# Low-rank second products from gathered adapter rows: one matmul per block instead of two

## The chip, the cores and the metric

The kernel runs on one core of a Trainium2 chip. Its metric is the device time of one execution in microseconds (us). Before the change the median of 3 runs is 657.62 us (656.94 to 659.66); the execution that was profiled took 656.7 us.

The engines are TensorE (PE, with its weight loads as PEld), VectorE (DVE), ScalarE (ACT), GpSimd (POOL) and SyncE (SP, which here only issues DMAs).

## The reference

Two layers, each a convolution or mixing followed by a residual feed-forward with low-rank parts, on x of 32 batches x 64 rows x 1024 columns, all in float32. Cut to what matters:

```
y   = einsum('bsd,od->bso', c0, weight) + bias        # c0: grouped convolution of x, plus a context term
seg = searchsorted(lora_start_indices, arange(B), side='right') - 1
a   = clip(seg - 1, 0, 2)                             # adapter of a batch, 3 adapters of rank 16
lo  = einsum('bsr,bor->bso', einsum('bsd,brd->bsr', c0, lora_A[a]), lora_B[a])
x   = x + y + where(seg > 0, lo, 0)                   # first layer
x   = x + second_layer(x)                             # 1x1 mixing by a softmax, scores, top 16 of 64 experts, A, gates, B
```

The change is in the product with `lora_B` and in the bias. Each batch has at most one of the three adapters.

## The kernel before

The 32 batches go in 4 groups of 8: 8 batches x 64 rows are 512 tokens, held as 4 blocks t of 128. Group 0 has its own code (`first_group`), groups 1 to 3 run `group`. A group's stages on PE are: the convolution; the first feed-forward product with weights of 128 x 1024 (pieces); the mixing and the scores; the experts' A product; the experts' B product. In groups 1 to 3 the feed-forward products go in seven block products (`winograd`, 24 matmuls each, numbered by their first step). To get float32 accuracy a product has three matmuls, high x high, high x low and low x high; ACT makes the high part of an operand (a copy into fp32r) and DVE the low part (a subtraction), so each piece passes SP (DMA), ACT, DVE and PE.

Every engine works its instructions off in the order in which its block of the source gives them, and waits on semaphores (`s_...`) written out by hand. The order is fixed; nothing is planned at run time.

The adapter part of a group:

- `lora_first` (L1392): 16 matmuls give the products with all three adapters, 48 rows twice (rows 0 to 47 with the high part of A, 64 to 111 with its low part), for 512 tokens in one bank.
- `masked` on DVE (L910) multiplies with `lora_mask`, which POOL computed in `adapters` (L573, 14 small operations): a row is kept where the batch has that adapter.
- `lora_parts` on ACT (L674) writes the high part to `lora_s1` (112 rows; row 48 is 1 for the bias) and a copy to the upper rows of `lora_s2`; `lora_rest` on DVE (L917) writes the low part to the lower rows of `lora_s2`.
- `lora_second` (L1399) adds the adapter part and the bias to a bank of the feed-forward product: two matmuls for a block t and a half h of the 1024 output columns, with `lora_m1` (high part of B over all 48 adapter rows, and the bias) and `lora_m2` (high and low parts). There are 8 blocks and halves in a group. In group 0 the 4 of h = 0 come after piece 3 of `ffn_piece` (L1484), those of h = 1 within piece 7, one after each t. In groups 1 to 3 two stand after winograd 8, two and two after winograd 10, two after winograd 12.

`const_hi` (ACT, L740) and `const_lo` (DVE, L1054) make `lora_m1` and `lora_m2` once, in group 0, out of the loaded `lora_b`.

POOL does little: memsets, `adapters()` (L621), then `mix_weights(0)` (L601, 15 operations over 128 x 256), and a loop over groups with `onto_diagonal` (L616), which sets the left side for the mixing stage, and `mix_weights(g + 1)`, which starts with the first second product of the group. In DVE's order the batch items of the convolution (`conv_item`, `conv_lo`) come first in a group; in group 1 DVE also has a combination of weights (`combine(3)`, `combined_lo(3, .)`) beside its usual work. `choose` is the selection of the top 16 experts.

Of the kernel before, what the change touches and what calls it, by code (L numbers as in the profile page):

```python
# [24 lines left out]
F32 = mybir.dt.float32  # L25
F32R = mybir.dt.float32r
I32 = mybir.dt.int32
ALU = mybir.AluOpType
# [3 lines left out]
P = 128  # L32
# [37 lines left out]
def adaln_ffn_kernel(nc, conv_x, x, taps, pieces, first_consts, hidden_w, later_consts, lora_a, lora_b,  # L70
                     starts, wr, expand, spread, out):
    with ExitStack() as ctx:
# [28 lines left out]
        lora_m1 = sb("lora_m1", [P, L], F32R)  # L101
        lora_m2 = sb("lora_m2", [P, L], F32R)
# [36 lines left out]
        lora_h, score_t, gate_t = small, small, small[0:KR_E, :]  # L139
        lora_a_raw = small[:, 0:PH * LORA].rearrange("p (k m) -> p k m", m=LORA)  # L140
# [67 lines left out]
        s_lora_lo = sem("s_lora_lo")  # L208
        s_ffn = sem("s_ffn")
# [21 lines left out]

        kept = nc.dram_tensor("kept", (16, 2, P, L), F32, kind="Internal").ap()
# [81 lines left out]
        def _(sp):  # L314
# [88 lines left out]
            def first_group():  # L403
# [14 lines left out]
                sp.wait_ge(s_const_hi, 4)  # L418
# [146 lines left out]
        def _(pool):  # L565
            pool.memset(ones[:, :], 1.0).then_inc(s_ones, 1)
            pool.memset(lora_a_r[:, :, :].bitcast(F32), 0.0).then_inc(s_ones, 1)
            pool.memset(lora_s2[:, :].bitcast(F32), 0.0).then_inc(s_ones, 1)
            pool.wait_ge(s_ones, 3)
            pool.memset(lora_s2[96:P, :].bitcast(F32), 1.0).then_inc(s_ones, 1)  # L570
            pool.wait_ge(s_ones, 4)

            def adapters():  # L573
# [25 lines left out]
                then(pool.tensor_scalar(lora_mask[:, :], high, 2.0, acol, ALU.subtract, ALU.is_equal))  # L599
# [21 lines left out]
            adapters()  # L621
            pool.wait_ge(s_att, 4)
# [3 lines left out]
            pool.wait_ge(s_ones, 5)  # L626
            for g in range(GROUPS):

                pool.wait_ge(s_conv, g * GB + 1)
                onto_diagonal()  # L630
                if g < GROUPS - 1:

                    pool.wait_ge(s_ffn, g * 8 + 1)
                    pool.wait_ge(s_bd, 2 * g + 2)
                    mix_weights(g + 1)

        @block.scalar
        def _(act):
# [74 lines left out]
            def first_group():  # L713
# [26 lines left out]
                def const_hi(n):  # L740
                    if n != 2:
                        act.wait_ge((s_lora_a, s_lora_b, None, s_wr)[n], 16)
                    if n == 0:
                        act.wait_ge(s_ones, 4)
                    to, of = ((lora_a_r[:, :, 0:LORA], lora_a_raw), (lora_m1[:, :], lora_b_stage),
                              (lora_m2[0:LORA_LO, :], x1[0:LORA_LO, 1, :]), (wr_r[:, :, 0:KR_E], wr_raw))[n]
# [24 lines left out]
                for n in range(1, 4):  # L771
                    const_hi(n)
# [5 lines left out]
                lora_parts(0)  # L778
                split_first(5)
# [47 lines left out]
            def group(g, last):  # L827
# [13 lines left out]
                lora_parts(g)  # L841
                next_split(8)
# [43 lines left out]
        def _(dve):  # L886
            dve.wait_ge(s_ones, 4)
# [29 lines left out]
            def lora_rest(g):  # L917
                dve.wait_ge(s_lora_s, 2 * g + 1)
                dve.wait_ge(s_lora_masked, g + 1)
                dve.tensor_tensor(lora_s2[0:LORA, :], lora_h[0:LORA, :], lora_s1[0:LORA, :].bitcast(F32),  # L920
                                  ALU.subtract).then_inc(s_lora_lo, 1)
# [93 lines left out]
            def first_group():  # L1015
# [12 lines left out]

                def softmax_max():
# [24 lines left out]
                def const_lo(n):  # L1054

                    dve.wait_ge(s_const_hi, (1, 2, 4)[n])
# [11 lines left out]
                for b in range(GB):  # L1068
# [9 lines left out]
                    if b == 1:  # L1078
                        rest_of_context()
                    if b == 4:  # L1080
# [15 lines left out]
                dve.wait_ge(s_adapter, 14)  # L1096
# [268 lines left out]
        def _(pe):  # L1365
# [33 lines left out]
            def lora_second(h, t, bank, start):  # L1399
                pe.matmul(banks[bank][:, :], lora_s1[0:LORA_M, t * P:(t + 1) * P],  # L1400
# [398 lines left out]
```

## Time and profile before

| what | value |
|---|---|
| median of 3 runs | 657.62 us (656.94 to 659.66) |
| profiled execution | 656.7 us, of which the span is 654.9 us |
| PE busy | 648.1 us (99%), 3197 matmul records |
| PEld busy | 537.7 us (82%) |
| DVE busy | 451.4 us (69%) |
| ACT busy | 214.0 us (33%) |
| POOL busy | 73.8 us (11%) |
| DMA | 157.98 MB, mean 241 GB/s |

Busy time is the time in which an engine has an instruction under way; the span is from the first to the last instruction. Matmuls overlap each other, so the mean duration of one (395 ns) is longer than the interval between two starts. The profile's clock row gives the TensorE clock that was granted, as a share of the full 2.4 GHz.

### The profile page before, as it was taken

What the parts mean: (1) busy time and instruction counts of PE and PEld (TensorE: products, weight loads), DVE (VectorE), ACT (ScalarE), POOL (GpSimd) and SP (SyncE); (2) the same over time, 40 slices, a digit from 0 to 9 for tenths busy, and PEclk for the clock granted to TensorE, in tenths of its full rate; (3) what the DMA queues carried; (4) which work ended last, traced back from release to release, by engine and by line L of the source; (5) the groups of instructions that cost most, each with busy time, mean ns of one, the idle gap of its engine ahead of it and who ended that gap; (6) DMA issues with size and microseconds to landing.
All of it is one profiled execution on the core that took longest, in us unless ns stands there. A gap on an engine that the chain in (4) does not pass through costs nothing.

```text
span 654.9 us, 8354 instructions
## 1 busy us (share of the span) xinstructions
PE 648.1 (99%) x3197; PEld 537.7 (82%) x3197; DVE 451.4 (69%) x690; ACT 214.0 (33%) x275; POOL 73.8 (11%) x91
## 2 busy tenths in 40 slices
PE   9999999999999999999999999999999999999997
PEld 8878888888897788888889788888879888888885
DVE  2859469549377788558769758636967856665785
ACT  2714135233144024335115312333423421433420
POOL 1598200000000160000000042000000000000000
PEclk9999999999999999999999999999999999999999
DMA  8587714986969926776976682287797664037795
GB/s 303 210 293 279 299 50 144 356 246 218 392 228 379 356 100 260 280 223 245 366 275 220 261 318 97 102 225 245 290 325 264 273 248 184 0 118 203 211 345 221
DMA packets 51594, 157.98 MB, mean 241 GB/s; under 512 B 5488, under 2 KB 6384, under 8 KB 51568
## 3 DMA queue, kind: packets, MB, share of 16 engines
q1 hardware_dynamic: 46240, 148.05, 62.7%
q10 hardware_dynamic: 5328, 9.61, 4.8%
q8 instruction: 13, 0.21, 0.1%
q14 instruction: 13, 0.11, 0.1%
HBM read 131.94 MB, written 25.71 MB: 241 GB/s over the span
## 4 chain that ended last, share of the span: by engine, by line
PE 91%; DVE 3%; DMA 3%; issue 1%; SPq 1%; ACT 0%; DVEq 0%
PE bank L1374 25%; PE bank L1376 24%; PE bank L1375 24%; PE bank L1388 9%; PE bank L1408 3%; DMA piece_lo<-kept 2%; PE bank L1395 2%; PE bank L1414 1%; PE bank L1402 1%; PE bank L1400 1%; PE bank L1415 1%; DVE x L925 1%; DMA gate<-hidden_w 1%; DVE u_lo L1012 1%; DVE work L932 1%
## 5 line engine op out<-in xcount | busy, mean ns | idle before, releaser
L893 DVE TENSOR_TENSOR piece_lo<-raw,piece_hi 128x1024 fp32r<-128x1024 f32 x60 | 74.1, 1239 | 90.0 <-ACT piece_hi L647 89.8
L647 ACT ACTIVATE piece_hi<-raw 128x1024 fp32r<-128x1024 f32 x60 | 63.4, 1058 | 147.1 <-PE bank L1376 103.2
L1374 PE MATMUL bank<-piece_hi,u_hi 128*128 128x512 f32 x272 | 107.9, 397 | 0.0
L1376 PE MATMUL bank<-piece_hi,u_lo 128*128 128x512 f32 x272 | 107.3, 395 | 0.0
L1375 PE MATMUL bank<-piece_lo,u_hi 128*128 128x512 f32 x272 | 107.3, 394 | 0.0
L1374 PE MATMUL bank<-v_hi,piece_hi 128*128 128x512 f32 x256 | 101.8, 398 | 0.0
L1376 PE MATMUL bank<-v_hi,piece_lo 128*128 128x512 f32 x256 | 101.1, 395 | 0.0
L1375 PE MATMUL bank<-v_lo,piece_hi 128*128 128x512 f32 x256 | 101.0, 394 | 0.0
L1374 PE MATMUL bank<-piece_hi,v_hi 128*128 128x512 f32 x192 | 76.0, 396 | 0.8 <-DMA piece_lo<-kept 0.8
L1376 PE MATMUL bank<-piece_hi,v_lo 128*128 128x512 f32 x192 | 75.8, 395 | 0.0
L1375 PE MATMUL bank<-piece_lo,v_hi 128*128 128x512 f32 x192 | 75.8, 395 | 0.0
L652 ACT ACTIVATE u_hi<-work 128x512 fp32r<-128x512 f32 x64 | 40.1, 631 | 87.6 <-DVE work L988 50.8
L925 DVE TENSOR_TENSOR x<-x,bank 128x512 f32<-128x512 f32 x86 | 54.3, 679 | 17.0 <-PE bank L1402 12.7
L1374 PEld LDWEIGHTS bank<-piece_hi,u_hi 128*128 128x128 f32 x272 | 51.2, 188 | 12.4 <-issue 0.5
L1376 PEld LDWEIGHTS bank<-piece_hi,u_lo 128*128 128x128 f32 x272 | 51.2, 188 | 12.0
L1375 PEld LDWEIGHTS bank<-piece_lo,u_hi 128*128 128x128 f32 x272 | 51.2, 188 | 11.8
L1388 PE MATMUL bank<-toep,conv_in 128*128 128x128 f32 x512 | 59.2, 276 | 0.2 <-DMA toep<-taps 0.2
L1388 PEld LDWEIGHTS bank<-toep,conv_in 128*128 128x128 f32 x512 | 58.2, 192 | 0.8 <-DMA toep<-taps 0.4
L1376 PEld LDWEIGHTS bank<-v_hi,piece_lo 128*128 128x128 f32 x256 | 48.2, 188 | 11.5
L1375 PEld LDWEIGHTS bank<-v_lo,piece_hi 128*128 128x128 f32 x256 | 48.2, 188 | 11.0
L1374 PEld LDWEIGHTS bank<-v_hi,piece_hi 128*128 128x128 f32 x256 | 48.2, 188 | 10.9
L899 DVE TENSOR_TENSOR u_lo<-work,u_hi 128x512 fp32r<-128x512 f32 x64 | 43.7, 686 | 15.1 <-ACT u_hi L652 13.8
(143 smaller groups left out, 800.7 us busy)
## 6 DMA issues: line engine op xcount, KB each, us to landing
raw<-pieces SPq DMA_DIRECT2D x76, 512.0 KB, 5.5
piece_hi<-kept SPq DMA_DIRECT2D x48, 512.0 KB, 4.7
piece_lo<-kept SPq DMA_DIRECT2D x48, 512.0 KB, 5.8
x<-x SPq DMA_DIRECT2D x16, 512.0 KB, 5.3
gate_x<-gates ACTq DMA_DIRECT2D x32, 256.0 KB
out<-x SPq DMA_DIRECT2D x32, 256.0 KB, 4.8
conv_in<-conv_x SPq DMA_DIRECT2D x15, 516.0 KB, 7.1
conv_in<-pieces SPq DMA_DIRECT2D x12, 512.0 KB, 8.8
```

The lines of the kernel that those rows point to most:

```text
L647: act.activation(piece_hi[:, n % SLOTS, :], raw[:, r % RAWS, :], ACT.Copy).then_inc(s_piece_hi, 1)
L652: act.activation(to, of, ACT.Copy).then_inc(s_hi, 1)
L893: dve.tensor_tensor(piece_lo[:, n % SLOTS, :], raw[:, r % RAWS, :], piece_hi[:, n % SLOTS, :].bitcast(F32), ALU.subtract).then_inc(s_piece ...
L899: dve.tensor_tensor(to, of, hi, ALU.subtract).then_inc(s_lo, 1)
L925: dve.tensor_tensor(half, half, of, ALU.add).then_inc(done, 1)
L932: dve.tensor_tensor(work[:, c, :], banks[bank][:, :], mixb_bc[:, :, :].rearrange("p b c -> p (b c)"), ALU.add).then_inc(s_item, 1)
L1374: pe.matmul(to, left_hi, right_hi, start=first, stop=False)
L1375: pe.matmul(to, left_hi, right_lo, start=False, stop=False)
L1376: return pe.matmul(to, left_lo, right_hi, start=False, stop=last)
L1388: mm = pe.matmul(banks[bank][:, cg * P:(cg + 1) * P], conv_in[:, b, cg, h:h + Q], toep[:, cg, 1 - h, :], start=(h == 0), stop=(h == 1))
L1395: mm = pe.matmul(banks[bank][0:LORA_M, :], lora_a_r[:, k, :], part[:, k, :], start=(k == 0 and part is u_hi), stop=(k == NCH - 1 and part ...
L1408: mm = pe.matmul(banks[bank][:, t * P:(t + 1) * P], x1[:, t, c * P:(c + 1) * P], blockdiag[:, t, :], start=True, stop=True)
```

## The change

The products with `lora_B` take one matmul instead of two. Its left side, `lora_s1`, has 128 rows, 64 for the even and 64 for the odd batches of each block, of which a batch fills its own 64 and leaves the others zero. The 64 rows of a batch are: 16 x 3 for its one adapter (the parts that meet the high, the low and the high part of B), and two for the bias. A matmul with a matrix of zeros and ones (`place`, 128 x 112, built by POOL in the tile of `ones`) puts the rows of `lora_s2` there, and two ACT copies bring them from the bank to `lora_s1`. The right side is `lora_m`, four slots of 128 x 512, each filled by an indirect DMA from a table in DRAM (`lora_rows`, 2 halves x 160 rows x 512) by row numbers that POOL computes from the batches' adapters. POOL writes the table by 12 DMAs. A slot is filled for one block t and one half h, and filled again when the matmul that reads it is done: 8 gathers of 256 KB a group, 32 in all. DVE computes a row number's base (`row_numbers`) after its second convolution item.

```diff
+            def placement():
+                first, second = agg_part[:, 0, 0:RANK], agg_part[:, 0, RANK:2 * RANK]
+                halves = place_r[:, :].rearrange("p (b j) -> p b j", b=2)
+                pool.wait_ge(s_p_att, 2)
+                pool.memset(place[:, :], 0.0).then_inc(s_place, 1)
...
+                pool.wait_ge(s_place, 7)
+            def store_rows():
+                pool.wait_ge(s_const_hi, 2)
+                pool.wait_ge(s_const_lo, 2)
+                for h in range(2):
...
+                    for part, rows in ((0, lora_m1[0:LORA, cols]), (1, lora_m2[LORA_LO:LORA_M, cols]),
+                                       (2, lora_m1[0:LORA, cols])):
+                        pool.dma_start(by_adapter[:, part * RANK:(part + 1) * RANK, :],
+                                       rows.bitcast(F32)).then_inc(s_rows, 16)
...
+                pool.wait_ge(s_rows, 16 * 12)
+            def gather(g, h, t, slot):
+                at = g * NT + t
+                pool.indirect_dma_start(lora_m[:, slot, :].bitcast(F32), None,
+                                        lora_rows.rearrange("h r n -> (h r) n"),
+                                        bass.IndirectOffsetOnAxis(ap=lora_row[:, at:at + 1], axis=0),
+                                        element_offset=h * 160 * HALF).then_inc(s_gather[slot], 16)
...
             adapters()
+            store_rows()
+            for t in range(NT):
+                gather(0, 0, t, (t + 2) % 4)
+            gathered(1)
+            placement()
             pool.wait_ge(s_att, 4)
             mix_weights(0)
...
                 onto_diagonal()
+                pool.wait_ge(s_bd, 2 * g + 2)
+                if g == 0:
+                    pool.wait_ge(s_ffn, 4)
+                    for t in range(NT):
+                        gather(0, 1, t, t)
+                    pool.wait_ge(s_ffn, 8)
+                else:
+                    for pair in range(2):
+                        pool.wait_ge(s_ffn, g * 8 + 2 * pair + 2)
+                        for s in range(2):
+                            gather(g, 1 - pair, 2 + s, 2 * pair + s)
                 if g < GROUPS - 1:
-                    pool.wait_ge(s_ffn, g * 8 + 1)
-                    pool.wait_ge(s_bd, 2 * g + 2)
+                    for pair in range(2):
+                        pool.wait_ge(s_ffn, g * 8 + 2 * pair + 6)
+                        for s in range(2):
+                            gather(g + 1, 1 - pair, s, 2 * pair + s)
+                    gathered(2 * g + 3)
                     mix_weights(g + 1)
...
             def lora_parts(g):
                 act.wait_ge(s_lora_masked, g + 1)
-                act.activation(lora_s1[0:LORA_M, :], lora_h[0:LORA_M, :], ACT.Identity,
-                               bias=ecol[0:LORA_M, 0:1]).then_inc(s_lora_s, 1)
-                act.activation(lora_s2[LORA_LO:LORA_M, :], lora_h[0:LORA, :], ACT.Copy).then_inc(s_lora_s, 1)
+                act.activation(lora_s2[0:LORA_LO, :], lora_h[0:LORA_LO, :], ACT.Identity,
+                               bias=ecol[0:LORA_LO, 0:1]).then_inc(s_lora_s, 1)
+            def lora_placed(g, bank):
+                act.wait_ge(s_lora_placed, g + 1)
+                for b in range(2):
...
+                    act.activation(lora_s1[rows, :].rearrange("p (t b c) -> p t b c", b=2, c=C)[:, :, b, :], of,
+                                   ACT.Copy).then_inc(s_lora_rows, 1)
...
+                def row_numbers():
+                    dve.wait_ge(s_later, 16)
...
-            def lora_second(h, t, bank, start):
...
+            def lora_place(g, bank):
+                pe.wait_ge(s_lora_lo, g + 1)
+                pe.matmul(banks[bank][:, :], place_r[0:LORA_M, :], lora_s2[0:LORA_M, :], start=True,
+                          stop=True).then_inc(s_lora_placed, 1)
+            def lora_second(gathered, t, slot, bank, start):
+                pe.wait_ge(s_gather[slot], gathered)
+                pe.matmul(banks[bank][:, :], lora_s1[:, t * P:(t + 1) * P], lora_m[:, slot, :], start=start,
                           stop=True).then_inc(s_ffn, 1)
...
+                        if n == 3 and t == NT - 1:
+                            pe.wait_ge(s_place, 7)
+                            lora_place(0, 5)
...
                     if n == 3:
-                        pe.wait_ge(s_lora_s, 2)
...
+                        pe.wait_ge(s_lora_rows, 2)
                         for t in range(NT):
-                            lora_second(0, t, t, False)
+                            lora_second(16, t, (t + 2) % 4, t, False)
```

Further edits: `adapters` gets 9 more operations on POOL, the row numbers (DVE waits for 22 counts of `s_adapter` instead of 14); `const_hi` loses one of its four ACT copies; `lora_rest` is two DVE operations instead of one; `lora_placed` stands behind `lora_parts` on ACT, in group 0 before `split_first(5)`, later before `next_split(8)`. In groups 1 to 3 the placement matmul stands between winograd 4 and winograd 6 and waits for `s_lora_lo`; PE waits for `s_lora_rows` before winograd 8. One of POOL's opening memsets goes.

## Rows read from the trace of the kernel before

**Rows 1.** Page, parts 1 and 2: PE's busy time, its granted clock.
```profile
PE 648.1 (99%) x3197; PEld 537.7 (82%) x3197; DVE 451.4 (69%) x690; ACT 214.0 (33%) x275; POOL 73.8 (11%) x91
PEclk9999999999999999999999999999999999999999
```

**Rows 2.** Page, part 4: the chain that ended last, by engine.
```profile
PE 91%; DVE 3%; DMA 3%; issue 1%; SPq 1%; ACT 0%; DVEq 0%
```

**Rows 3.** PE's waits: who waited, for whom, total us, times, longest.
```profile
PE bank L1374 <- DMA piece_lo<-kept: 0.8, 1, 0.8
```

**Rows 4.** Timeline of PE (start, duration in us): first and 25th matmul.
```profile
53.43 0.40 PE L1374 MATMUL bank<-piece_hi,u_hi 128*128 128x512 f32 x1
...
59.00 0.39 PE L1374 MATMUL bank<-piece_hi,u_hi 128*128 128x512 f32 x1
```

**Rows 5.** Stretches: PE, PEld, DVE, ACT, POOL busy, PE clock, DMA share.
```profile
226.00:232.00 6.00, 6.00 (x27) 4.86 (x27) 3.48 (x5) 1.06 (x1) 5.31 (x7) 1.00 0.79 317
240.00:258.00 18.00, 17.39 (x106) 14.89 (x105) 16.64 (x23) 8.59 (x13) 0.04 (x1) 1.00 0.57 223
```

**Rows 6.** Tile lora_s: duration ns min/median/max, first and last start us.
```profile
L1400 PE MATMUL bank<-lora_m,lora_s x32: 391/398/402, 51.6 to 554.6; 112*128 112x512 f32 x32
L676 ACT ACTIVATE lora_s<-small,consts x4: 723/724/726, 46.9 to 524.4; 112x512 fp32r<-112x512 f32 x4
```

**Rows 7.** Timeline of POOL in group 0.
```profile
17.46 0.42 POOL L586 CAST starts_f<-starts_i 128x4 f32<-128x4 int32 x1 [14.70 <-DMA consts<-later_consts]
...
25.45 0.93 POOL L599 TENSOR_SCALAR lora_mask<-left,consts 128x32 f32<-128x32 f32 x1
32.00 1.59 POOL L609 TENSOR_TENSOR agg<-att_pair,consts 128x256 f32<-128x256 f32 x1 [5.62 <-DVE att_pair L1048]
...
34.69 1.60 POOL L613 TENSOR_TENSOR agg<-agg,agg_part 128x256 f32<-128x256 f32 x1
...
47.23 0.74 POOL L613 TENSOR_TENSOR agg<-agg,agg_part 128x256 f32<-128x256 f32 x1
...
48.62 2.64 POOL L619 COPY blockdiag<-agg 64x256 f32<-64x256 f32 x2
```

**Rows 8.** Timeline of PE, and chain of waits: piece 3, mixing stage.
```profile
50.15 0.40 PE L1374 MATMUL bank<-piece_hi,u_hi 128*128 128x512 f32 x1
77.77 3.57 PE bank L1408 x32
```

**Rows 9.** Timelines of DVE and ACT in group 0.
```profile
14.93 0.67 DVE L903 TENSOR_TENSOR work<-bank,cond_bc 128x512 f32<-128x512 f32 x1
...
31.88 1.22 DVE L1060 TENSOR_TENSOR lora_m<-x,lora_m 64x1024 fp32r<-64x1024 f32 x1
26.07 1.99 ACT L747 ACTIVATE lora_m<-x 128x1024 fp32r<-128x1024 f32 x2
```

**Rows 10.** Timeline of SP's queue, and DMA issues (KB, us to landing).
```profile
3.42 0.43 SPq L390 DMA_DIRECT2D gate<-hidden_w  x1
gates<-small ACTq DMA_DIRECT2D x4, 128.0 KB, 2.6
out<-x SPq DMA_DIRECT2D x32, 256.0 KB, 4.8
```

**Rows 11.** Timeline of PE's weight loads at the start.
```profile
0.99 4.90 PEld L1370 LDWEIGHTS bank<-ones 128*128 128x128 f32 x24 [0.99 <-POOL ones L566]
5.81 0.97 PEld L1388 LDWEIGHTS bank<-toep,conv_in 128*128 128x128 f32 x8
```

**Rows 12.** The chain of waits, and the timeline of ACT, in group 2.
```profile
363.18 3.73 PE bank L1395 x16
369.72 1.06 ACT L647 ACTIVATE piece_hi<-raw 128x1024 fp32r<-128x1024 f32 x1 [0.68 <-PE bank L1376]
```

**Rows 13.** Timeline of DVE in groups 1 and 3, four x adds.
```profile
233.17 4.05 DVE L925 TENSOR_TENSOR x<-x,partial 128x512 f32<-128x512 f32 x4
547.53 2.49 DVE L925 TENSOR_TENSOR x<-x,partial 128x512 f32<-128x512 f32 x4
```

More of the change, by code:

```diff
@@ L27 @@
 I32 = mybir.dt.int32
+U32 = mybir.dt.uint32
 ALU = mybir.AluOpType
@@ L139, in adaln_ffn_kernel @@
         lora_h, score_t, gate_t = small, small, small[0:KR_E, :]
+        place = ones[:, :]
+        place_r = place.bitcast(F32R)
+        lora_m1, lora_m2 = (lora_m[:, 2 * n:2 * n + 2, :].rearrange("p s n -> p (s n)") for n in range(2))
         lora_a_raw = small[:, 0:PH * LORA].rearrange("p (k m) -> p k m", m=LORA)
@@ L208, in adaln_ffn_kernel @@
         s_lora_lo = sem("s_lora_lo")
+        s_lora_rest = sem("s_lora_rest")
+        s_lora_placed = sem("s_lora_placed")
+        s_lora_rows = sem("s_lora_rows")
+        s_gather = [sem(f"s_gather{slot}") for slot in range(4)]
+        s_row = sem("s_row")
+        s_rows = sem("s_rows")
+        s_place = sem("s_place")
         s_ffn = sem("s_ffn")
@@ L567, in _ @@
             pool.memset(lora_a_r[:, :, :].bitcast(F32), 0.0).then_inc(s_ones, 1)
[L568 to L571, printed above, removed]
+            pool.memset(lora_s1[:, :].bitcast(F32), 0.0).then_inc(s_ones, 1)
             def adapters():
@@ L598, in adapters @@
                 then(pool.tensor_tensor(high, high, low, ALU.add))
-                then(pool.tensor_scalar(lora_mask[:, :], high, 2.0, acol, ALU.subtract, ALU.is_equal))
+                then(pool.tensor_scalar(lora_mask[:, :], high, 2.0, acol, ALU.subtract, ALU.is_equal), False)
+                least_row, quarter_row, row = (stat[:, 1, n:n + 1] for n in range(3))
+                then(pool.tensor_scalar(low, high, 2.0, 0.0, ALU.subtract, ALU.max), False)
+                then(pool.tensor_scalar(least_row, acol, 3.0, 2.0, ALU.is_ge, ALU.mult), False)
@@ new lines, in adapters @@
+                then(pool.tensor_scalar(quarter_row, acol, 2.0, 32.0, ALU.is_ge, ALU.mult))
+                pool.wait_ge(s_row, 1)
+                then(pool.tensor_tensor(row, quarter_row, stat[:, 0, 0:1], ALU.add), False)
+                then(pool.tensor_scalar(low, low, least_row, 48.0, ALU.max, ALU.mult))
+                then(pool.tensor_scalar(low, low, row, None, ALU.add))
+                for b in range(2):
+                    rows = slice(b * C, (b + 1) * C)
+                    then(pool.tensor_copy(lora_row[rows, :], low[rows, :].rearrange("p (t b) -> p t b", b=2)[:, :, b]))
@@ new lines, in gather, with gathered @@
+            def gather(g, h, t, slot):
[4 more added lines that the diff above has]
+                                        element_offset=h * 160 * HALF).then_inc(s_gather[slot], 16)
+            def gathered(count):
+                for slot in range(4):
+                    pool.wait_ge(s_gather[slot], 16 * count)
@@ L770, in first_group @@
                         logits_exp()
-                for n in range(1, 4):
+                for n in range(1, 3):
                     const_hi(n)
@@ L778, in first_group @@
                 lora_parts(0)
+                lora_placed(0, 5)
                 split_first(5)
@@ L841, in group @@
                 lora_parts(g)
+                lora_placed(g, 0)
                 next_split(8)
@@ L1079, in first_group @@
                         rest_of_context()
+                        row_numbers()
                     if b == 4:
@@ L1674, in group @@
                 for s in range(2):
-                    lora_second(0, 2 + s, 1 - s, False)
+                    lora_second(g * 32 + 32, 2 + s, 2 + s, 1 - s, False)
                 def h_of(c, ks):
```

83 lines of the change are left out of this document (54 added, 29 removed).

## The prediction

> **What bounds the kernel now.** I read the page's first two parts, then the chain of waits, the waits of TensorE (PE), and the timelines of the places that the diff touches. PE is busy 99% of 654.9 us at a granted clock of 1.00 [rows 1]; the chain is PE's for 91% [rows 2]; PE's longest wait in the steady groups is 0.8 us [rows 3]. So a matmul that disappears is worth its issue interval, not its 395 ns (these overlap): 24 matmuls from 53.43 to 59.00 us [rows 4] make 5.57 / 24 = 0.232 us. For the same reason each wait that is new on PE counts in full; there is no slack for it to fall into. The one stretch that another engine sets is the mixing stage of group 1: in 240 to 258 us PE has 17.39 of 18.00 us and DVE 16.64 [rows 5].
>
> **What the change removes.** 64 second-product matmuls (two lines of 32, the first in [rows 6]) become 32, and one placement matmul comes with each of 4 groups: 28 fewer, 28 x 0.232 = 6.5 us, 1.6 us a group. On ACT two operations of which the longer has 0.72 us [rows 6] become one of that kind and two half-size copies; on DVE one operation becomes two. Weight and moving shapes stay near 128 x 512, so I keep the interval.
>
> **What it adds in group 0: a chain on POOL that PE waits for.** Now POOL ends the adapter masks at 25.45 + 0.93 = 26.4 us, mixes weights from 32.00 to 47.97, and PE wants nothing of it until the mixing stage at 77.77 [rows 7, 8]. After, the placement matmul (before the last quarter of piece 3) waits for s_place 7, and ahead of that on POOL stand, in order:
> - 9 more mask operations. 14 took 17.46 to 26.4, 0.64 each, so they end near 32.1. Hidden: the store waits longer.
> - The store waits for const_lo 1, on DVE at 31.88 + 1.22 = 33.1 [rows 9]. DVE itself is late: row_numbers waits after the second convolution item (14.93) for later_consts, which POOL sees at 17.46 [rows 7, 9]. DVE stops 2.5 us and its later gaps (it still waits three times for PE in this stage) win back half; one ACT copy less (half of 1.99 us for two, [rows 9]) wins back more. I take +0.8: the store starts at 33.9. On PE this costs up to 0.7 us at the last quarter of piece 0, but the stall below swallows it.
> - 12 DMA issues on POOL. No row shows one. Bounds: the 0.43 us of an SP issue, and the 1.60 us of a POOL add [rows 7, 10]. I take 1.0, the middle, since neither is nearer: 12.0 us, to 45.9. Then the last must land: 2.6 us is the fastest of the DMAs by kind [rows 10]; I take 3.0, near it, since these are small: 48.9.
> - 4 gathers (256 KB each) at 1.0, and landing. Bounds of landing: 2.6 and, for 256 KB, 4.8 us [rows 10]; since SP, whose loads wait for DVE, has little left to issue while PE stands, 3.0: 55.9.
> - 7 small operations at 0.3, half the 0.64 above since they are at most half as wide (the memset aside): 2.1 us. The placement is ready at T = 58.0.
> PE arrives at 50.15 [rows 8] and stalls 58.0 - 50.2 = 7.8 us. With both low ends T = 33.9 + 5.2 + 2.6 + 1.7 + 2.6 + 2.1 = 48.1: no stall. With the high ones T = 33.9 + 19.2 + 4.8 + 6.4 + 4.8 + 2.1 = 71.2: a stall of 21 us. Behind the waiting matmul PE has everything; ACT too waits in its order (lora_placed stands before split_first 5), and so does DVE.
>
> **A second stall of the same chain.** From T, PE has 1 + 6 + 4 + 3 x 24 + 6 = 89 matmuls, 20.6 us, to the first product of the second half, which needs slot 0 of the second gathers (the two ACT copies, about 0.45 each, are ready before the 6 matmuls are through). POOL has from T: mixing weights 16.0 (as now), memset and diagonal copies 3.3 [rows 7], one issue 1.0, landing 3.4: T + 23.7. PE stalls another 3.1, and ends the piece 22 matmuls later at T + 28.8 = 86.8, against 77.77 now: **+9.0 us in group 0**, the removed matmuls included.
> The granted clock is 1.00 in every row, but PE never stood for more than a microsecond, so no row shows a restart after 7.8 us of idleness. Nearest: the first 24 weight loads took 4.90 us, 0.204 each, the next 8 took 0.97, 0.121 each [rows 11]: a slow restart would lose at most 24 x 0.083 = 2.0 us, and here it would eat into the second stall. So 0 in the sum, 2.0 in the range.
>
> **Groups 1 to 3: the gathers.** A slot is free when the product that used it ends (R); the same slot is wanted 26 matmuls after the release, R + 5.9 us (slot 0 or 2) and R + 6.1 (slot 1 or 3). Issue 1.0, landing 4.0 (between 2.6 and 4.8; the DMA share is 0.79 at 226 to 232 us, [rows 5]): R + 5.1 and R + 6.1. So 0, just. With 1.6 and 4.8 the second comes at R + 8.1: 2.0 us a pair, two pairs a group, 12 us in all at the high end. The Trainium skill (DMA: Bandwidth & Descriptors, "Anatomy of one DMA") gives about 2.0 us plus the bytes at 436 GB/s for a DMA from GpSimd, an estimate of 2.6 us for 256 KB where the rows of this trace have 4.8; with 2.6 for every landing the sum would be 1.6 us lower.
> The gathered rows add 32 x 256 KB = 8.4 MB to 158 MB; PE's only DMA wait (0.8 us) may grow. I cost it 0.
>
> **ACT's order.** In group 2 ACT splits piece 8 at 369.72, while PE's first adapter product ends at 363.18 + 3.73 = 366.9 [rows 12] and winograd 4 24 matmuls later, at 372.5. After, lora_placed stands before both splits (pieces 8 and 9) and waits for PE at 372.5. Piece 8 is then split at 373.8 to 374.9, its rest on DVE at 376.1; PE wants it after 24 more matmuls, at 378.1. Piece 9: DVE's four adds between (2.5) put it at 379.8, wanted 12 matmuls on at 380.9. Hidden with 2.0 and 1.1 us to spare; cost 0, up to 1 a group if copies are slower.
>
> **POOL's mixing moved.** mix_weights(g+1) now runs beside the last second products, and it slows DVE: four x adds take 4.05 us beside it in group 1, 2.49 without it in group 3 [rows 13]: 0.4 each. After, it starts when the gathers have landed, some 8 us later, so beside the mixing stage. In groups 0 and 2 DVE has room: a chunk costs PE 8 short matmul records (32 are 3.57 us, [rows 8]) and 5 long ones, 0.89 + 1.16 = 2.05 us, and DVE two operations of 0.67 [rows 9], 1.7 with one of them slowed. In group 1, where DVE also has a weight combination, it gives back about what is won earlier: 6 + 3 operations, 0.4 us each, 3.6 us at most, against 2.2 us gained before and 1.6 of matmuls: I take 0 for this group, between -1.6 and +3. Groups 2 and 3 keep their 1.6: -3.2.
>
> **Sum.** +9.0 + 0 - 3.2 = +5.8 us. The profiled execution took 656.7 (its span 654.9 and 1.8 around it): 662.5. It lay 0.9 under the median of the runs, 657.6, so on the median's scale 663.4.
>
> **Rivals.**
> - Cheap issues on POOL: near 0.43 us each. For it: no POOL row has to do with a DMA, so nothing shows 1.0. Against it: 12 issues and two landings in a row must fit in 16 us. No stall: group 0 gives its 1.6 too, less 0.7 for DVE's wait: 657.6 - 0.9 - 3.2 = 653.5. Chance 0.13. This is the other side; it decides below (50.2 - 33.9 - 2.6 - 2.6 - 2.1) / 16 = 0.56 us an issue.
> - Issues about 0.65, and group 1 losing 2 to 3 us on DVE: T = 52.4, group 0 +3.4, the sum +2.2 to +3.2, 660 to 661. It needs two middling costs. Chance 0.13.
> - The gathers late in every group: issue 1.3 or more, T = 62.8 (group 0 +14) and 1 us at each of 6 pairs. For it: the margin above is zero. 657.6 + 14 - 3.2 + 6 = 674. Against: the gathers have 5.9 us where the DMA rows of that size have 4.8. Chance 0.17.
> - The forecast, 659 to 669: 0.57.
>
> **Numbers.** I can tell 0.5% (3.3 us) from nothing. Faster: the first rival, 0.13. Same (654.3 to 660.9): the second, and the low edge of the forecast, 0.19. Slower: 0.68. The range for 8 in 10 is 654 to 675: it drops the fastest end of the first rival and the far part of the third. The forecast's own is 659 to 669.
>
> **What would show it.** A gap on PE before the last quarter of piece 3 near 50 us, ended by POOL, and ACT idle in the same microseconds; a smaller one in piece 7 ended by a DMA; the mixing stage of group 0 beginning near 87; 32 second products and 4 placements; POOL's DMA issues of about 1 us; groups 2 and 3 shorter by 1.6 us each. It is wrong if PE passes 50 us without a gap, or if the groups after the first lose time at lora_second.

## The result, and the profile after

The changed kernel takes 678.35 us (median of 6 runs, 675.26 to 679.25) against 657.26 us of the kernel before (6 runs, 655.57 to 659.66): ratio 1.0317, 95% interval 1.0287 to 1.0346. It is slower by 21 us, where 663.4 were forecast and 675 was the top of the range.

The page and the waits of PE, after (the answers to [rows 1 to 3]):

```profile
PE 648.4 (96%) x3169; PEld 535.7 (79%) x3169; DVE 454.5 (67%) x696; ACT 213.0 (31%) x278; POOL 120.3 (18%) x149
PEclk9996979999999999999999999999999999999999
```

```profile
PE bank L1513 <- POOL ones L640: 9.1, 1, 9.1
PE bank L1518 <- DMA lora_m<-lora_rows,lora_row: 8.3, 6, 4.0
PE bank L1529 <- DVE v_lo L999: 2.3, 3, 1.3
PE bank L1486 <- DMA piece_lo<-kept: 1.5, 2, 0.8
```

28 matmul records are gone and PE is busy for as long as before. At 0.232 us each they would have saved 6.5 us; some 4.5 of these go into matmuls at a lower clock, for the clock row, 9 everywhere before, has a 6 and a 7 in its fourth and sixth slices. The rest of the loss is waiting: two kinds of wait that did not exist before, one for the placement and six for gathered rows, make 17.4 us.

The milestone that I use in all that follows is the start of the score transposes, once in each group. PE's timeline, after; the kernel before has them at 94.81, 259.01, 415.77 and 572.25, with 82.65 us behind the last:

```profile
111.70 0.60 PE L1546 MATMUL bank<-consts,small 128*128 128x128 f32 x4
279.69 0.60 PE L1546 MATMUL bank<-consts,small 128*128 128x128 f32 x4
436.89 0.60 PE L1546 MATMUL bank<-consts,small 128*128 128x128 f32 x4
593.90 0.60 PE L1546 MATMUL bank<-consts,small 128*128 128x128 f32 x4
```

Group 0 loses 16.9 us, group 1 (milestone to milestone) 3.8, group 2 0.4, group 3 0.5; the end gains 0.2. The sum is 21.4, the difference of the spans (676.3 and 654.9).

POOL's timeline in group 0, which is the chain that PE waits for (answers to [rows 7]):

```profile
33.78 2.12 POOL L653 DMA_DIRECT2D lora_rows<-lora_m  x3 [3.91 <-DVE wr_r L1171]
35.90 0.53 POOL L655 DMA_DIRECT2D lora_rows<-lora_m  x1
...
40.34 0.52 POOL L659 DMA_DIRECT2D lora_rows<-lora_m  x1
49.65 2.10 POOL L666 DMA_INDIRECT lora_m<-lora_rows,lora_row  x1 [8.80 <-DMA lora_rows<-lora_m]
52.05 0.97 POOL L666 DMA_INDIRECT lora_m<-lora_rows,lora_row  x1 [0.30 <-issue]
...
58.29 0.20 POOL L627 MEMSET ones<- 128x128 f32 x1 [2.77 <-DMA lora_m<-lora_rows,lora_row]
...
80.17 1.02 POOL L666 DMA_INDIRECT lora_m<-lora_rows,lora_row  x1 [0.27 <-POOL blockdiag L693]
```

The 12 store issues take 7.1 us, 0.59 each; then POOL stands 8.8 us until the table has landed. PE's timeline at the two stalls (answers to [rows 8]):

```profile
59.91 0.79 PE L1513 MATMUL bank<-lora_s,ones 112*128 112x512 f32 x1 [9.08 <-POOL ones L640]
60.50 0.63 PE L1486 MATMUL bank<-piece_hi,u_hi 128*128 128x512 f32 x1
60.93 0.63 PE L1487 MATMUL bank<-piece_lo,u_hi 128*128 128x512 f32 x1
...
87.09 0.79 PE L1518 MATMUL bank<-lora_m,lora_s 128*128 128x512 f32 x1 [4.02 <-DMA lora_m<-lora_rows,lora_row]
...
94.48 3.73 PE L1523 MATMUL bank<-blockdiag,x 128*128 128x128 f32 x32
```

Stretches of the same kernel: each engine's busy time, then PE's clock, the DMA share and GB/s:

```profile
52.00:56.00 4.00, 0.00 (x0) 0.00 (x0) 0.07 (x1) 0.00 (x0) 2.86 (x3) 0.80 0.50 183
56.00:60.00 4.00, 0.09 (x1) 0.09 (x1) 0.00 (x0) 0.00 (x0) 1.47 (x8) 0.50 0.27 79
60.00:64.00 4.00, 4.00 (x10) 3.13 (x11) 1.36 (x2) 3.21 (x5) 3.77 (x5) 0.50 0.00 2
64.00:68.00 4.00, 4.00 (x18) 3.23 (x17) 4.00 (x3) 4.00 (x5) 3.77 (x4) 0.92 0.67 227
84.00:88.00 4.00, 0.91 (x2) 0.82 (x3) 0.39 (x2) 0.00 (x0) 1.20 (x1) 0.64 1.03 414
88.00:92.00 4.00, 4.00 (x11) 3.03 (x11) 1.36 (x2) 0.00 (x0) 0.00 (x0) 0.51 1.02 417
```

The granted clock falls to 0.50 (1.2 GHz) within the stall and stays there for some microseconds behind it: matmuls then start 0.43 us apart (60.50, 60.93) and not 0.232. In this view it shows as "PE busy 4.00" with 10 or 11 matmuls instead of 18 or 19. The last line of the timeline is the start of the mixing stage, at 94.5.

### The profile page after: what moved, and what is told of

The parts are those of the page before. It is cut to its first block, busy times and chain, and to the rows that moved or that the text cites. A ratio compares the mean times of both kernels' runs of the same rounds, so it can differ in the third digit from the quotient of the medians.

```text
span 676.3 us, 8380 instructions
## 1 busy us (share of the span) xinstructions
PE 648.4 (96%) x3169; PEld 535.7 (79%) x3169; DVE 454.5 (67%) x696; ACT 213.0 (31%) x278; POOL 120.3 (18%) x149
## 4 chain that ended last, share of the span: by engine, by line
PE 69%; DMA 15%; DVE 7%; POOL 5%; issue 2%; ACT 1%; SPq 1%; ACTq 0%; DVEq 0%; POOLq 0%
PE bank L1486 18%; PE bank L1487 18%; PE bank L1488 18%; PE bank L1500 7%; DMA gate_x<-gates 5%; DMA lora_m<-lora_rows,lora_row 4%; PE bank L1523 3%; DMA raw<-pieces 2%; DMA piece_lo<-kept 2%; POOL agg L687 1%; DMA lora_rows<-lora_m 1%; PE bank L1507 1%; POOL agg_part L685 1%; PE bank L1518 1%; PE bank L1529 1%
## 5 line engine op out<-in xcount | busy, mean ns | idle before, releaser
L1486 PE MATMUL bank<-piece_hi,v_hi 128*128 128x512 f32 x192 | 75.9, 395 | 1.5 <-DMA piece_lo<-kept 1.5
L666 POOL DMA_INDIRECT lora_m<-lora_rows,lora_row x32 | 34.1, 1066 | 177.7 <-PE bank L1518 162.3
```

Source lines behind the costliest of these rows:

```text
L666: pool.indirect_dma_start(lora_m[:, slot, :].bitcast(F32), None, lora_rows.rearrange("h r n -> (h r) n"), bass.IndirectOffsetOnAxis(ap=lor ...
L1486: pe.matmul(to, left_hi, right_hi, start=first, stop=False)
```

## The experiments

My theory after the result: (a) group 0 is a chain on POOL (stores, landing, gathers, mixing, gathers again), and it is late by its landings; (b) PE loses more than it stands, by the clock; (c) from group 1 on the regathered slots come 1 to 2 us late; (d) group 1 loses on DVE beside the moved mixing. The rivals were that 17 us of group 0 are simply waiting, and that the groups' loss is spread over the loads.

All times are in us; "group n" is the interval between milestones, less that of the kernel before (164.20, 156.76, 156.48), and group 0 the milestone less 94.81. The profiled runs differ by some 2.5 us in where the first group starts, by waits on the first loads, so group 0 is uncertain by that. The groups come from one profiled run each, and that run is not always near the median: it took 670.1 us in a_table_given and 675.2 in a_warm, the fastest of their runs.

| kernel | median | ratio, 95% interval | group 0 | 1 | 2 | 3 |
|---|---|---|---|---|---|---|
| after | 678.35 | 1.0317 [1.0287, 1.0346] | +16.9 | +3.8 | +0.4 | +0.5 |
| c_stall_short | 665.01 | 1.0108 [1.0078, 1.0137] | +8.5 | -0.7 | +1.3 | 0.0 |
| c_stall_long | 669.14 | 1.0187 [1.0163, 1.0211] | +12.7 | -0.5 | -0.2 | +0.1 |
| a_table_given | 673.05 | 1.0256 [1.0223, 1.0289] | +8.3 | +2.8 | +2.3 | +0.4 |
| a_hold_loads | 675.94 | 1.028 [1.026, 1.03] | +14.8 | +3.0 | +0.4 | +2.0 |
| a_warm | 677.74 | 1.0326 [1.031, 1.0343] | +14.1 | +3.7 | +0.5 | +0.5 |
| a_pair_later | 671.29 | 1.0204 [1.018, 1.0228] | +17.1 | +1.6 | -2.1 | -1.3 |
| a_no_regather | 671.11 | 1.0211 [1.0196, 1.0226] | +18.6 | +1.7 | -2.1 | -1.9 |
| a_mix_early | 677.31 | 1.0295 [1.026, 1.033] | +17.8 | +2.4 | +1.3 | +0.3 |
| a_group0 | 667.55 | 1.0145 [1.012, 1.0169] | +4.6 | +3.6 | +2.0 | +0.8 |
| all_three | 657.69 | 1.0019 [0.9999, 1.0039] | +5.0 | -1.5 | -1.7 | -1.8 |
| all_early | 657.7 | 1.0015 [0.9997, 1.0033] | +4.9 | -0.7 | -2.1 | -1.8 |
| all_last | 656.59 | 0.9991 [0.9975, 1.0007] | +3.5 | -1.8 | +0.3 | -1.7 |

### What a stall of PE costs

The kernel before, with a wait for POOL where the placement will stand: 8 memsets (c_stall_short), 22 (c_stall_long).

```
+                if g == 0:
+                    pool.wait_ge(s_bd, 2)
+                    for n in range(8):            # 22 in the long one
+                        pool.memset(expd[:, :, :], 0.0).then_inc(s_pad, 1)
+                        pool.wait_ge(s_pad, n + 1)
...
+                        if n == 3 and t == NT - 1:
+                            pe.wait_ge(s_pad, 8)
```

> The kernel before, with one thing added: TensorE waits at the place of the placement matmul (last quarter of piece 3) for 8 memsets on GpSimd that end near 54.3 us, a stall of about 4 us. Theory (a stall costs its length, and a long one also costs a slow restart): 4.0 us plus nothing or up to 2.4 us, +4 to +6.5 us. Rival (the stages after it have slack that takes a stall back): under +2 us.

> The same with 22 memsets, ending near 59.8 us, where the changed kernel's placement is ready: a stall of about 9.5 us. Theory: 9.5 us plus a restart at a granted clock of 0.5 for about 4.5 us, which costs 2.4 us here because no second stall hides it: +12 us. Rival (the clock costs nothing or the slack takes it back): +9.5 us or less.

PE's timeline of the short and of the long one, and stretches of the short one:

```profile
56.02 0.80 PE L1380 MATMUL bank<-piece_hi,u_hi 128*128 128x512 f32 x1 [5.44 <-POOL expd L635]
```

```profile
60.73 0.79 PE L1380 MATMUL bank<-piece_hi,u_hi 128*128 128x512 f32 x1 [9.08 <-POOL expd L635]
```

```profile
52.00:56.00 4.00, 0.00 (x0) 0.00 (x0) 4.00 (x4) 2.35 (x3) 3.50 (x9) 0.86 0.50 156
56.00:60.00 4.00, 3.98 (x9) 3.14 (x10) 2.63 (x3) 0.96 (x1) 0.06 (x1) 0.50 0.99 352
60.00:64.00 4.00, 4.00 (x15) 3.21 (x14) 3.87 (x5) 0.10 (x1) 3.77 (x5) 0.79 1.03 420
```

A stall of 5.44 us moves the milestone by 8.5, one of 9.08 by 12.7. Of these 0.3 and 1.3 are a late start; from the moment at which the waiting matmul was due, PE stands 5.6 and 9.3 us, and what is left is 2.6 and 2.1 us. That is what the slow matmuls behind the stall lose: 13 in the short one and 10 in the long one, 0.43 us apart instead of 0.232. So each stall costs its length and 2.1 to 2.6 us more, which do not grow with it. The medians agree: +7.9 and +12.1 us, the first above its band of +4 to +6.5 (the stall was longer than planned), the second as forecast. No table, gather or placement is in these kernels, so the drop of the clock belongs to the standing PE. The Trainium skill (TensorE: Matmul & The Clock Gate, "Wait — 56ns, not 53.3ns?") has matmuls of 512 columns 426.7 ns apart at 1.2 GHz; the trace agrees, with 0.43 us.

a_warm asks the same of the changed kernel, by dummy matmuls in the stalls.

```
+                            for _ in range(36):
+                                pe.matmul(banks[7][:, :], u_hi[:, 0, 0:P], u_hi[:, 0, :], start=True, stop=True)
                             pe.wait_ge(s_place, 7)
...
+                            pe.wait_ge(s_f, 4)
+                            for _ in range(26):
+                                pe.matmul(banks[0][:, :], u_hi[:, 0, 0:P], u_hi[:, 0, :], start=True, stop=True)
```

> The changed kernel with 36 dummy matmuls ahead of the placement's wait and 26 ahead of the second half's first second product (into banks whose contents are not read): at the 0.232 us of a matmul they take 8.4 and 6.0 us, which is within the stall of 9.08 us and within what the second one becomes when no slow stretch stands ahead of it (4.02 + 2.4). Theory 1 (the clock falls because TensorE is idle, and stays low for some microseconds behind the stall): the granted clock stays at 1.00 through both, the first wait still ends near 59.9 and the second near 87.1 (POOL's chain and the landing set them), and only the matmuls behind the second run faster: 22 matmuls in 5.1 instead of 7.4 us, time 2 to 2.5 us below the changed kernel's 678.4, so 676. Theory 2 (the low clock comes of something else, such as the loads): the clock dips all the same, no change, within 1 us.

Its timeline of PE and its stretches:

```profile
50.47 8.37 PE L1607 MATMUL bank<-u_hi 128*128 128x512 f32 x36
59.70 0.50 PE L1513 MATMUL bank<-lora_s,ones 112*128 112x512 f32 x1 [0.86 <-POOL ones L640]
```

```profile
52.00:58.00 6.00, 6.00 (x29) 4.93 (x27) 0.00 (x0) 0.00 (x0) 2.75 (x3) 1.00 0.62 175
88.00:92.00 4.00, 4.00 (x20) 3.08 (x18) 1.44 (x3) 0.00 (x0) 0.00 (x0) 1.00 1.00 407
```

The trace answers as theory 1 said: clock 1.00 throughout, and the milestone 2.8 us earlier (forecast 2 to 2.5). The times do not: the median is 0.6 us less where 2 to 2.5 were expected, the ratio to the kernel before is no lower (1.0326 against 1.0317, the intervals overlap), and the profiled run was the fastest of its five. That the clock falls by idleness is shown; that it was worth 2.3 us of the 21 rests on the traces of this run and of the two kernels above, and the times of a_warm do not resolve it.

### Where group 0's chain is late

a_table_given lets SP fill the table early by plain copies of the loaded matrix, in place of POOL's 12 stores (so the adapters' part is computed with other numbers). a_hold_loads keeps everything and makes SP's loads of x, and all that SP issues behind them, wait for the stores.

```
+                sp.dma_start(lora_rows[h, 0:64, :], lora_b[0:64, ...]).then_inc(s_rows, 16)    # a_table_given
+                sp.dma_start(lora_rows[h, 64:160, :], lora_b[0:96, ...]).then_inc(s_rows, 16)
...
+                pool.wait_ge(s_rows, 64)
+                return                     # in store_rows: the 12 stores behind it are never issued
```
```
+                sp.wait_ge(s_rows, 16 * 12)                                                    # a_hold_loads
                 for h in range(2):
                     for th in range(2):
                         load_x(0, th, h)
```

> The changed kernel without the 12 stores of the table: SP copies rows of lora_b into it at the start, so the adapter products are computed with other numbers. Theory (group 0 is lost to the chain store, landing, gather, placement on GpSimd): no stall at the placement, none or a short one in piece 7, clock 1.00 throughout; the mixing stage of group 0 near 77 us instead of 94.5, and 659 to 662 us in all. Rival (gathers and their contention with the loads cost the time): above 668 us.

> The changed kernel with SP's four loads of x (2 MB, issued at 34 to 37 us) held until the table's stores have landed. Theory (the stores land 8.8 us after the last issue because they share full queues with these loads): they land 4 to 6 us earlier, the placement is ready at 54 to 56, and the time falls by 4 to 6 us, to 673. Rival (the landing of GpSimd's stores is long by itself): the placement stays at 59 to 60 and the time at 678.

POOL's timeline in a_hold_loads, and in a_table_given:

```profile
45.32 1.07 POOL L667 DMA_INDIRECT lora_m<-lora_rows,lora_row  x1 [3.40 <-DMA lora_rows<-lora_m]
...
55.91 0.20 POOL L628 MEMSET ones<- 128x128 f32 x1 [5.74 <-DMA lora_m<-lora_rows,lora_row]
```

```profile
41.59 0.95 POOL L671 DMA_INDIRECT lora_m<-lora_rows,lora_row  x1 [0.30 <-issue]
48.04 0.20 POOL L630 MEMSET ones<- 128x128 f32 x1 [5.50 <-DMA lora_m<-lora_rows,lora_row]
```

The stores land 3.4 us after their last issue when SP's loads are held, 8.8 beside them (in the changed kernel the DMA share is 0.93 to 1.08 from 34 to 48 us). Then the held loads meet the gathers, which land after 5.7 us and not 2.8, and the placement is ready at 57.5, not at the 54 to 56 that I expected. So contention makes the landing, and holding the loads only hands it on: 2.4 us gained in the median (4 to 6 expected) of the 5.4 by which the stores land sooner. Without stores the first stall shrinks to 1.8 us, yet I had expected 659 to 662 and got 673: the second stall stayed, 4.3 us, for it hangs on POOL's mixing and on a landing that goes through full queues, not on the stores. That was my second miss on the same quantity, the landing.

a_group0 takes the chain off PE's path by order alone: POOL does the placement matrix and five steps of the mixing while the stores land, and PE's second products of h = 0 stand in piece 5.

```
+            mix_weights(0, range(5))
+            pool.wait_ge(s_rows, 16 * 12)
+            for t in range(NT):
+                gather(0, 0, t, t)
+            mix_weights(0, range(5, KC))
...
+                        if n == 5:
+                            lora_second(16, t, t, t, False)
```

> The changed kernel with group 0's preparation in another order: POOL does the placement matrix's inputs and a part of the mixing while the table's stores land, then gathers, the rest of the mixing, and the second products of group 0 are put later in TensorE's order (after the half of piece 4 and inside piece 5), so that neither the placement nor the regathered rows are waited for. Theory 1 (what the change costs is the two stalls of group 0 and the slow clock behind them, 16.7 us of 20.7): group 0's score transposes stand near 96 to 98 us instead of 111.7, and the time is 661 to 665 us. Theory 2 (the stores and gathers are a burden wherever they stand, by VectorE, ScalarE or the loads they delay): 670 to 676 us. If a stall is left, the rows show which wait has it.

Group 0 goes from +16.9 to +4.6, the time from 678.4 to 667.6 (2.6 above the expected band). Theory 1 holds in the main, and one stall of 3.73 us, which ends at 75.45 with the landing of the second gathers, is left.

### Groups 1 to 3

a_pair_later moves the second products of the first regathered pair into the middle of the next winograd piece; a_no_regather drops the four gathers inside a group (adapter part with other numbers); a_mix_early puts POOL's mixing ahead of the gathers.

```
+                def third_pair():                                                # a_pair_later
+                    for s in range(2):
+                        lora_second(g * 32 + 32, 2 + s, s, 4 + s, True)
-                winograd(12, (1, 0), u_hi, u_lo, block_of(1, 1), False)
+                winograd(12, (1, 0), u_hi, u_lo, block_of(1, 1), False, third_pair)
```
```
-                            gather(g, 1 - pair, 2 + s, 2 * pair + s)             # a_no_regather
+                            pass
```
```
                 pool.wait_ge(s_bd, 2 * g + 2)                                    # a_mix_early
+                if 0 < g < GROUPS - 1:
+                    mix_weights(g + 1)
```

> The changed kernel, but in groups 1 to 3 the second products that wait for the regathered slots 0 and 1 (second half, blocks 2 and 3) are put half a piece later, into the middle of the twelfth first-product piece. In the changed kernel TensorE waits there 1.27 us in group 1, 1.11 in group 2 and 1.90 in group 3 (the wait for lora_m). Theory: the regathered rows land 1 to 2 us after TensorE needs them, and half a piece (about 3 us) covers this: the waits go, time 674 to 676 us. Rival: the wait moves with it (the gathers' landing is held back by the loads that run beside them): 678 us, no change.

> The changed kernel without the four gathers inside each of groups 1 to 3 that refill a slot for the other half; the products use what the slots hold, so the result has other numbers in the adapters' part. Theory 1 (groups 1 to 3 lose by waiting for those refills): the waits of 1.27, 1.11 and 1.90 us go, as they did with the pair half a piece later, and the time is as that version's, 671 to 673 us. Rival (part of that version's gain of 7 us was the order of the products, not the wait): 674 to 675 us.

> The changed kernel, but the program lists POOL's weight mixing for the next group (k = 0 to 15) straight after the diagonal blocks, ahead of the in-group gathers and the next group's, for groups 1 and 2. In the changed kernel the mixing for group 2 starts at 264.56 and lies beside VectorE's own mixing stage, whose v_lo adds take 1.64 to 1.76 us there instead of 1.22, and TensorE waits 2.3 us for it. Theory 1 (the shared work of POOL and VectorE is what group 1 loses by): the mixing ends before that stage, the 2.3 us go, the milestone of group 1's score transposes stands 1.5 to 3 us earlier, time 675.5 to 677 us; the in-group gathers are later by the mixing and must still be there for the second half. Theory 2 (the in-group gathers come 18 us later and TensorE waits for them by more than that): 680 us and more. Rival: no change, within 1 us of 678.4.

PE's timeline of the changed kernel in group 1, POOL's there, and DVE's in the mixing stage:

```profile
252.52 0.93 PE L1518 MATMUL bank<-lora_m,lora_s 128*128 128x512 f32 x2 [1.27 <-DMA lora_m<-lora_rows,lora_row]
```

```profile
245.96 1.32 POOL L666 DMA_INDIRECT lora_m<-lora_rows,lora_row  x1 [47.45 <-PE bank L1518]
247.58 0.96 POOL L666 DMA_INDIRECT lora_m<-lora_rows,lora_row  x1 [0.30 <-issue]
...
264.56 0.62 POOL L683 TENSOR_TENSOR agg<-att_pair,consts 128x256 f32<-128x256 f32 x1 [2.57 <-DMA lora_m<-lora_rows,lora_row]
```

```profile
262.88 1.22 DVE L1116 TENSOR_TENSOR u_lo<-conv_in,u_hi 128x1024 fp32r<-128x1024 f32 x1 [0.25 <-ACT u_hi L810]
...
274.89 1.76 DVE L1116 TENSOR_TENSOR u_lo<-conv_in,u_hi 128x1024 fp32r<-128x1024 f32 x1
276.57 1.10 DVE L999 TENSOR_TENSOR v_lo<-work,v_hi 128x512 fp32r<-128x512 f32 x1
```

The first pair's waits are 1.27, 1.11 and 1.90 us in the three groups. Moving the pair or dropping the gathers gives the same 7 us (671.3 and 671.1), so it was the wait and not the order. For the moved pair I had expected 2 to 4. Without it groups 2 and 3 are 1.3 to 2.1 us shorter than in the kernel before, near the 1.6 that 7 fewer matmuls promised. a_mix_early takes the v_lo waits of group 1 from 2.3 to 0.2 us and the group from +3.8 to +2.4, but its gathers come later: in group 2 PE waits 1.9 us for them instead of 1.1, and 0.5 for the convolution's work, and that group goes from +0.4 to +1.3. The time is 677.3, between theory 1's band (up to 677.0) and the rival's (from 677.4): the mechanism is shown in group 1, its worth in the whole is not resolved. DVE's u_lo operations (128x1024; the text on record calls them v_lo) take 1.22 us ahead of POOL's mixing and 1.64 to 1.76 beside it, and v_lo (128x512) 0.67 to 1.11; in a_mix_early, with the mixing out of the way, the same operations take 1.22 to 1.23 and 0.68 throughout. POOL's adds take up to 1.60 beside DVE instead of 0.74.

### Together

all_three joins a_group0, a_mix_early and a_pair_later. all_early further issues group 0's second gathers ahead of the last mixing step; all_last instead puts the four second products of h = 1 behind piece 7's products.

```
-            mix_weights(0, range(5, KC))                                         # all_early
+            mix_weights(0, range(5, KC - 1))
+            for t in range(NT):
+                pool.wait_ge(s_ffn, t + 1)
+                gather(0, 1, t, t)
+            mix_weights(0, range(KC - 1, KC))
```
```
+                    if n == 7:                                                   # all_last
+                        for t in range(NT):
+                            lora_second(32, t, t, 4 + t, False)
```

> The three edits together: group 0's other order, the mixing ahead of the gathers, and the pair half a piece later. If they are independent the gains add: 14 to 17 us, 2 to 3 and 2 to 3 below 678.4, so 655 to 660 us, which is as fast as or faster than the kernel before (657.3). Rival: the removed 64 matmuls give nothing in groups 1 to 3, because VectorE's mixing stage and the loads set the end there; then 661 to 665 us, slower than before by some 0.5 to 1.2 per cent.

> The three edits together, and group 0's gathers for the second half moved ahead on POOL: straight after two more steps of the mixing (each behind its slot's second product), with the last step, the clearing of the blocks and the diagonal behind them. In the version with three edits they are issued at 68.19 to 72.98, behind the last steps and the diagonal, and TensorE waits 3.77 us at 75.13 for the first and runs at half clock behind it. Theory: issued from about 63 on they land by 69 to 73, ahead of the seventh piece; the wait and the slow stretch go, the mixing of group 0 starts near 77 instead of 82.6, and the time is 651 to 654 us, under the 657.2 of the kernel before. Rival: the diagonal blocks, now behind the landing, are what TensorE waits for instead (they end near 76 to 79), or the earlier transfers delay the loads beside them: 656 to 658 us.

> The version with three edits, and group 0's four second products of the second half issued together behind the seventh piece's products instead of one behind each quarter of it, so that the first is needed near 75.5 instead of 71.4 (its rows are there at 75.1). Theory 1 (what is left of the change's cost is the wait of 3.77 us and the half clock behind it): the wait shrinks to under 1 us per product, the mixing stage starts near 79.5 instead of 82.6 and group 0's transposes stand near 97 instead of 99.8: 654 to 655.5 us. Rival (VectorE sets the stage then: its piece_lo of the next piece, which waits for a load, ended at 79.0 in the version with three edits, and the x adds are queued behind it; moving the gathers alone gave nothing): 656.5 to 658 us, no change to the 657.7.

PE's timeline in all_three, then all_early, then all_last; and DVE's in all_three:

```profile
75.13 0.79 PE L1522 MATMUL bank<-lora_m,lora_s 128*128 128x512 f32 x1 [3.77 <-DMA lora_m<-lora_rows,lora_row]
```

```profile
75.46 0.50 PE L1523 MATMUL bank<-lora_m,lora_s 128*128 128x512 f32 x1 [0.57 <-DMA lora_m<-lora_rows,lora_row]
```

```profile
77.90 0.51 PE L1522 MATMUL bank<-lora_m,lora_s 128*128 128x512 f32 x1 [0.85 <-DMA lora_m<-lora_rows,lora_row]
79.23 0.50 PE L1522 MATMUL bank<-lora_m,lora_s 128*128 128x512 f32 x1 [0.83 <-DVE x L1033]
```

```profile
77.80 1.23 DVE L1180 TENSOR_TENSOR piece_lo<-raw,piece_hi 128x1024 fp32r<-128x1024 f32 x1 [10.14 <-ACT piece_hi L856]
```

The three edits took 10.8, 1.0 and 7.1 us off the median one by one, and together 20.7, inside the expected 655 to 660: the gains add. In group 1, all_three is at -1.5 where a_pair_later alone is at +1.6, so the earlier mixing is worth up to 3 us there (group 0's order differs too). All three versions stand level with the kernel before. all_early shrinks the stall of 3.77 us to 0.57 and gains nothing, where 651 to 654 was expected: in its trace DVE waits 10.8 us for a loaded piece (10.1 in all_three) with the x adds queued behind it, and PE then waits 1.7 us for DVE in the mixing stage. This is the rival that the earlier transfers delay the loads. In the kernel before that piece is split at 71.5; in these it is at 75.9 to 79.8, as its load lands later, though SP issues it at 62.4 in all_three and at 63.6 before. What delays it was not tested; the second gathers (1 MB) share the queues with it, and these are at a share of 1.0 from 60 to 80 us (in the kernel before until 76). all_last ends at 656.59, in the rival's band and not in the expected 654 to 655.5, ratio 0.9991 [0.9975, 1.0007]: no version here beats the kernel before by more than the measurement can tell. What groups 1 to 3 gain (5.0 us in all_three, 3.2 in all_last), group 0 takes (5.0 and 3.5).

## Why the prediction was wrong, step by step

The sign and the places of group 0 were right: a stall ended by POOL before the last quarter of piece 3, a second one ended by a DMA in piece 7. Two things failed: the size of the terms in group 0, the landings above all, and the claim that the gathers of groups 1 to 3 are hidden. The loss of the profiled run exceeds the forecast's 5.8 us by 15.6: 7.9 in group 0, 3.8 in group 1, 4.1 in groups 2 and 3 (+0.9 where -3.2 was forecast), less 0.2 at the end. The prediction's own sign of being wrong, time lost at lora_second after the first group, is in the trace. The mixing stage of group 0 starts at 94.5, where 86.8 was forecast and 77.8 stood before. These 16.7 us are the forecast's 9.0, and:

- **T = 59.9, not 58.0 (+1.9).** Two errors that nearly cancel. 12 issues at 1.0 us were 0.59 each (-4.9). "Then the last must land ... I take 3.0" was 8.8 us (+5.8): I took the landing from the fastest kind of DMA [rows 10] and did not ask what the queues carry at that time. Four gathers took 5.9 us and not 4.0 (+1.9: 2.10 for the first, then 1.25 apart); their landing was 0.2 less, the small operations 0.5 less. With 0.59 an issue and the other terms as forecast T would have been 53.1, a stall of 2.9 us. The stores' issues came close to what the first rival wanted (it decides below 0.56, for stores and gathers alike), and the landing defeated it. The mask operations ahead are 8 and not 9, and ended at 29.9 and not 32.1; this was hidden, as said. I also took 4.8 us as the upper bound of a 256 KB landing; the DMA view of the kernel before has other kinds of that size at 7.7 to 11.0, and 2 KB at 8.7, so landings of 8.8 us were there to be read:

```profile
cond_bc<-spread SPq DMA_DIRECT2D x3, 256.0 KB, 7.7
blockdiag<-wr SPq DMA_DIRECT2D x1, 256.0 KB, 11.0
starts_i<-starts SPq DMA_DIRECT2D x1, 2.0 KB, 8.7
```

- **The second gathers at T + 27.2, not T + 23.7 (+3.5).** The mixing took 18.2 us, not 16.0 (the steps before 62.7 took 0.62 to 0.74 us, with DVE idle; DVE starts again at 62.64, and those up to 74 took 1.5 to 1.7 beside it); the memset and the diagonal were 1.3 cheaper; the gather landed 5.9 us after its issue, not 3.4, at a DMA share of 1.0.
- **"So 0 in the sum, 2.0 in the range" for the restart (+2.3).** That the loss behind the first stall is hidden in the second was right. The second stall has one of its own: 22 matmuls took 7.4 us and not 5.1. I priced the restart from the weight loads of the start [rows 11] and only once.
- **"So 0, just" for the gathers of groups 1 to 3.** The margin was zero and I took it as enough. Issue spacing 1.25 and landings up to 5 us gave waits of 1.1 to 1.9 us a group, and with what follows them 1.8 to 2.5, by a_pair_later.
- **Group 1 at 0, between -1.6 and +3.** +3.8: 1.3 by the gathers, 1.8 more by v_lo than before (2.3 against 0.5; the moved mixing, as described), and 0.9 by late work of the convolution stage, which I had not in the list and whose cause was not tested; against them stand the 1.6 of the matmuls. This makes 2.4; the other 1.4 us I cannot place.
- **The -1.6 of groups 2 and 3** was sound: -1.3 to -2.1 once the waits are gone. In the changed kernel it shows as +0.4 and +0.5.

The nearest rival was "the gathers late in every group" (674, chance 0.17): right that they are late, but it wanted 1.3 us for every issue. The gathers came near that (1.25); the 12 stores took 0.59, and group 0 lost its time in the landings. By the Trainium skill (DMA: Bandwidth & Descriptors, "Anatomy of one DMA") a gather would take an estimated 2.6 us; the traces here have 2.8 after an idle stretch and, beside other transfers, 5.5 (a_table_given), 5.7 (a_hold_loads) and 5.9 at a full DMA share.

## What to carry to other kernels

Price a DMA's landing by what the queues carry when it is issued (8.8 us here beside loads, 3.4 without), not by the fastest row of its kind; where stores and gathers stand in one chain ahead of a busy engine, each of them pays it. A stall on TensorE cost its length plus the slow matmuls behind it, once for each stall. A chain that is late is best taken off the path by order (other work of the same engine into its landings, its consumers later): here that was worth 20.7 us with no instruction removed, and it only paid back what the change had cost.

## What the hardware showed that I had not expected

- POOL issues a plain DMA in 0.51 to 0.62 us (0.91 for the first) and an indirect one of 128 rows mostly in 0.95, 1.25 apart; the first one took 2.10, and one in a_table_given 4.11.
- The granted clock is down to 0.50 (1.2 GHz) behind a stall of 4 to 9 us and comes back to 1.00 while PE works; 2.1 to 2.6 us were lost each time.
- The same small stores land in 3.4 us or in 8.8, by whether 512 KB loads are in the queues beside them.
